# A recurrence swept twice over its chunks: first sweep without a loop, and the input's products for two steps at a time

## The reference

```python
def _L0_ffn_ref(x, W, V, gamma, beta):
    Wx = jnp.einsum('bti,hi->bth', x, W)
    flat = Wx.reshape(B * T, H)
    mean = jnp.mean(flat, axis=0)
    var = jnp.var(flat, axis=0)
    Wx = ((flat - mean) * jax.lax.rsqrt(var + BN_EPS) * gamma + beta).reshape(B, T, H)
    Vt = V.T

    def step(yt, wx_t):
        yt = jax.nn.sigmoid(wx_t + yt @ Vt)
        return (yt, yt)
    ...
    _, ys = jax.lax.scan(step, y0, jnp.swapaxes(Wx, 0, 1))
    return jnp.swapaxes(ys, 0, 1)
...
t = t + _L0_ffn_ref(_ln_t(t), ...)
```

## Time and profile before

| | us |
|---|---|
| median of three runs | 303.04 |
| the three runs | 302.4, 303.04, 312.51 |
| span of the profiled execution (first to last instruction) | 300.2 |
| PE busy over the span | 231.0 |
| DVE busy | 223.3 |
| POOL busy | 150.0 |
| ACT busy | 117.7 |

### The profile page before, as it was taken

The page is one execution under the profiler, slowest core; times in us unless marked ns, Lnnn a source line. Parts: engine busy times, 40 slices in busy tenths (PEclk is TensorE's granted clock), DMA queues, the critical chain, the costliest instruction groups (busy, mean ns, idle before and its releaser), DMA issues.

```text
span 300.2 us, 4789 instructions
## 1 busy us (share of the span) xinstructions
PE 231.0 (77%) x1649; PEld 163.7 (55%) x1649; DVE 223.3 (74%) x384; ACT 117.7 (39%) x227; POOL 150.0 (50%) x223
## 2 busy tenths in 40 slices
PE   0285896868099799997969999795129999889893
PEld 0174782534044399995757869794119972333331
DVE  4999648978778600497893556899997999898893
ACT  3353533343423155555644637752303341231210
POOL 4443881368600088420519469945933528875100
PEclk9999996877789999999998999999655556999999
DMA  6200000000000000000000000000006982868311
GB/s 210 85 15 2 2 2 0 0 1 2 0 0 0 0 0 3 0 2 2 1 2 0 2 0 1 2 2 1 0 0 146 204 196 62 204 182 185 122 37 70
DMA packets 6636, 13.10 MB, mean 44 GB/s; under 512 B 2774, under 2 KB 3030, under 8 KB 6614
## 3 DMA queue, kind: packets, MB, share of 16 engines
q1 hardware_dynamic: 6470, 12.81, 16.8%
q10 hardware_dynamic: 144, 0.01, 0.0%
HBM read 2.32 MB, written 2.10 MB: 15 GB/s over the span
## 4 chain that ended last, share of the span: by engine, by line
DVE 40%; PE 36%; POOL 8%; issue 7%; ACT 5%; DMA 2%; DVEq 1%; SPq 1%; POOLq 0%; ACTq 0%
PE ps L1065 4%; PE ps L1061 4%; DVE var L372 4%; DVE sums L334 4%; PE ps L1483 3%; PE ps L654 3%; POOL x L875 3%; PE ps L1350 3%; PE ps L1368 2%; DVE gated L1958 2%; DMA raw<-in_L_conv_gi_b_dram 2%; PE ps L1248 2%; DVE squares L2094 2%; DVE xn L644 2%; PE ps L1462 1%
## 5 line engine op out<-in xcount | busy, mean ns | idle before, releaser
L654 PE MATMUL ps<-ident,xn 128*128 128x128 f32 x144 | 29.8, 345 | 20.0 <-DVE xn L644 10.5
L654 PEld LDWEIGHTS ps<-ident,xn 128*128 128x128 f32 x144 | 20.8, 179 | 32.8 <-issue 10.3
L875 POOL TENSOR_TENSOR x<-x,sg 128x512 f32 x16 | 22.0, 1390 | 9.2 <-DVE sg L2015 7.7
L1137 PE MATMUL ps<-ones_b,ones_h 128*128 128x512 bf16 x53 | 16.6, 465 | 10.4 <-ACT v_wrap L1584 7.5
L1958 DVE TENSOR_TENSOR gated<-ps,sg 128x512 f32 (+1 forms) x16 | 16.5, 1042 | 10.6 <-ACT sg L1635 10.5
L1098 ACT ACTIVATE gated_t<-ps,bn 128x128 f32<-128x128 f32 x54 | 16.9, 364 | 13.8 <-PE ps L1065 12.9
L372 DVE TENSOR_REDUCE var<-squares 128x32 f32<-128x1024 f32 (+1 forms) x18 | 19.6, 1090 | 2.2 <-ACT squares L340 1.4
L663 ACT ACTIVATE xt<-ps 128x512 f32<-128x512 f32 (+1 forms) x24 | 12.4, 525 | 22.1 <-PE ps L654 17.0
L1462 PE MATMUL ps<-gated,pick 96*128 96x512 bf16 x64 | 20.3, 427 | 0.1
L340 ACT ACTIVATE squares<-x 128x1024 f32<-128x1024 f32 x12 | 12.7, 1056 | 14.8 <-POOL x L875 11.2
L334 DVE TENSOR_REDUCE sums<-x 128x32 f32<-128x1024 f32 x12 | 14.5, 1211 | 4.2 <-DMA x<-in_x_dram 2.9
(11 more groups left out here) (282 smaller groups left out, 632.9 us busy)
## 6 DMA issues: line engine op xcount, KB each, us to landing
out_gate<-gated SPq DMA_DIRECT2D x32, 128.0 KB, 2.3
x<-gated SPq DMA_DIRECT2D x32, 128.0 KB, 2.4
x<-in_x_dram SPq DMA_DIRECT2D x4, 512.0 KB, 5.9
out_dram<-x SPq DMA_DIRECT2D x8, 256.0 KB, 2.0
e_full<-in_L_ffn_expert_b_dram SPq DMA_DIRECT2D x12, 1.0 KB
mask_a<-in_L_conv_mask_dram SPq DMA_DIRECT2D x1, 64.0 KB, 6.8
mask_c<-in_L_conv_mask_dram SPq DMA_DIRECT2D x1, 64.0 KB, 1.8
w_x<-in_L_ffn_expert_w_dram SPq DMA_DIRECT2D x1, 32.0 KB
```

The costliest lines, as they stand in the source:

```text
L654: ins = pe.transpose(bank(s)[:, t * P:(t + 1) * P], xn[:, s, t, :], ident[:, :])
L875: pool.tensor_tensor(v, v, sg[:, s, :], ALU.add).then_inc(pj.added, 1)
L1137: pe.matmul(bank(b).rearrange("p (k o) -> p k o", o=P), ones_h[:, :], ones_b[:, :].unsqueeze(1).to_broadcast([P, GROUP, P]), start=True, s ...
```

## The change

On TensorE both sweeps get code of their own. An input product takes two steps of one stream at once: 256 columns, written to the two halves of one bank (`pair_input`, `summed_at`); a stream's two banks alternate from pair to pair. The state products stay as they were, with 128 columns each. After both state products of a step one pair is issued, for stream 0 and stream 1 in turn (`pair_steps`). The first sweep has no loop any more. In the second sweep the pairs for steps 0 and 1 of both streams stand ahead of the wait for the first sweep's last states. ScalarE's activations keep their order and number and read the new places (`pairs_act`). The repeat loop keeps `sweep_pe` and `sweep_act`, which lose what only the two sweeps needed.

```diff
-        def sweep_pe(pe, stepped, state, base, first=False, begun=None, after=None):
+        def sweep_pe(pe, stepped, state, base):
...
-            begin = FIRST + 1 if first else 1
-            if not first:
...
-            if after:
-                for k in range(1, CHUNK):
-                    step(k, k % 2)
-                    if k in after:
-                        after[k]()
-                return
-            step(begin, begin % 2)
-            with pe.Fori((begin + 1) // 2, CHUNK // 2) as it:
...
+        def pair_at(k, begin):
+
+            n = k - begin
+            return 1 - (n // 2) % 2, P * (n % 2)
+
+        def summed_at(st, k, begin):
+
+            b, at = pair_at(k, begin)
+            return bank(2 + 2 * st + b)[:, at:at + P]
+
+        def pair_input(pe, st, k, begin):
+
+            n = min(2, CHUNK - k)
+            b, at = pair_at(k, begin)
+            pe.matmul(bank(2 + 2 * st + b)[:, 0:n * P], w_bs[:, :],
+                      x_cm[:, CHUNK * st + k:CHUNK * st + k + n, :].rearrange("p a i -> p (a i)"), start=True,
+                      stop=False, skip_group_check=True)
+
+        def pair_state(pe, st, k, begin, base):
+
+            pe.wait_ge(s_state[st], base + k)
+            pe.matmul(summed_at(st, k, begin), v_t[:, :], y_cm[:, CHUNK * st + k - 1, :], start=False,
+                      stop=True, skip_group_check=True).then_inc(s_step[st], 1)
+
+        def pair_steps(pe, k, begin, base, after={}):
+
+            for j in range(k, CHUNK):
+                st = (j - begin) % 2
+                for t in range(2):
+                    pair_state(pe, t, j, begin, base)
+                ahead = j - st + 2
+                if ahead < CHUNK:
+                    pair_input(pe, st, ahead, begin)
+                if j in after:
+                    after[j]()
+
+        def first_sweep_pe(pe):
+
+            k = FIRST + 1
+            for st in range(2):
+                pair_input(pe, st, k, k)
+                pair_state(pe, st, k, k, -FIRST)
+            pair_input(pe, 0, k + 2, k)
+            pair_steps(pe, k + 1, k, -FIRST)
+
+        def second_sweep_pe(pe, after):
+
+            last = y_cm[:, 2 * CHUNK - 1, :]
+            for st in range(2):
+                pair_input(pe, st, 0, 0)
+            for st in range(2):
+                pe.wait_ge(s_state[st], SWEPT)
+            pe.matmul(summed_at(0, 0, 0), v_next[:, :], last, start=False, stop=False, skip_group_check=True)
...
+            pair_input(pe, 0, 2, 0)
+            pair_steps(pe, 1, 0, SWEPT, after)
...
-            sweep_pe(pe, s_step, s_state, -FIRST, True)
+            first_sweep_pe(pe)
...
-            sweep_act(act, s_step, s_state, -FIRST, FIRST + 1)
-            sweep_act(act, s_step, s_state, SWEPT, kept=lambda: act.wait_ge(ends_kept, 1))
+            pairs_act(act, FIRST + 1, -FIRST)
+            pairs_act(act, 0, SWEPT, kept=lambda: act.wait_ge(ends_kept, 1))
```

More of the change, by code:

```diff
@@ L1082, in sweep_pe @@
-            if after:
-                for k in range(1, CHUNK):
-                    step(k, k % 2)
-                    if k in after:
-                        after[k]()
-                return
-            step(begin, begin % 2)
-            with pe.Fori((begin + 1) // 2, CHUNK // 2) as it:
+            last = y_cm[:, 2 * CHUNK - 1, :]
+            for st in range(2):
+                pe.matmul(summed(st, 0, 0), w_bs[:, :], x_cm[:, CHUNK * st, :], start=True, stop=False,
+                          skip_group_check=True)
@@ new lines, in sweep_pe @@
+            pe.matmul(summed(0, 0, 0), v_next[:, :], last, start=False, stop=False, skip_group_check=True)
+            pe.matmul(summed(0, 0, 0)[:, 1:P], v_wrap[:, :], last[:, 0:P - 1], start=False, stop=True,
+                      skip_group_check=True).then_inc(stepped[0], 1)
+            pe.matmul(summed(1, 0, 0), v_t[:, :], y_cm[:, CHUNK - 1, :], start=False, stop=True,
+                      skip_group_check=True).then_inc(stepped[1], 1)
+            step(1, 1)
+            with pe.Fori(1, CHUNK // 2) as it:
@@ L1090, in sweep_pe @@
                 for b in range(2):
                     step(2 * it + b, b)
-        def sweep_act(act, stepped, state, base, first=0, kept=None, looped=False):
+        def pair_at(k, begin):
[10 more added lines that the diff above has]
+                      stop=False, skip_group_check=True)
@@ new lines, in first_sweep_pe @@
+        def first_sweep_pe(pe):
[6 more added lines that the diff above has]
+        def second_sweep_pe(pe, after):
+            last = y_cm[:, 2 * CHUNK - 1, :]
+            for st in range(2):
+                pair_input(pe, st, 0, 0)
+            for st in range(2):
+                pe.wait_ge(s_state[st], SWEPT)
+            pe.matmul(summed_at(0, 0, 0), v_next[:, :], last, start=False, stop=False, skip_group_check=True)
+            pe.matmul(summed_at(0, 0, 0)[:, 1:P], v_wrap[:, :], last[:, 0:P - 1], start=False, stop=True,
+                      skip_group_check=True).then_inc(s_step[0], 1)
+            pe.matmul(summed_at(1, 0, 0), v_t[:, :], y_cm[:, CHUNK - 1, :], start=False, stop=True,
+                      skip_group_check=True).then_inc(s_step[1], 1)
+            pair_input(pe, 0, 2, 0)
+            pair_steps(pe, 1, 0, SWEPT, after)
@@ L1095, in step, with pairs_act, sweep_act @@
+        def pairs_act(act, begin, base, kept=None):
+            for k in range(begin, CHUNK):
+                if kept and k == CHUNK - 1:
+                    kept()
+                for st in range(2):
+                    act.wait_ge(s_step[st], base + k + 1)
+                    act.activation(y_cm[:, CHUNK * st + k, :], summed_at(st, k, begin), ACT.Sigmoid,
+                                   bias=bn[:, 9:10]).then_inc(s_state[st], 1)
+        def sweep_act(act, stepped, state, base):
             def step(k, b):
@@ L1099, in step @@
                                    ACT.Sigmoid, bias=bn[:, 9:10]).then_inc(state[st], 1)
[L1101 to L1109, removed]
+            with act.Fori(0, CHUNK // 2) as it:
+                for b in range(2):
+                    step(2 * it + b, b)
         def keep_ends(dve, signal):
@@ L1269, in _ @@
             pe.wait_ge(bn_dve, 4)
-            def first_swept():
-                for st in range(2):
-                    pe.wait_ge(s_state[st], SWEPT)
-            sweep_pe(pe, s_step, s_state, -FIRST, True)
+            first_sweep_pe(pe)
             def turn_y(q, st):
@@ L1290, in turn_quarter @@
                 turn_y(q, 1).then_inc(y_turn, 1)
-            sweep_pe(pe, s_step, s_state, SWEPT, begun=first_swept,
-                     after={GROUP * (q + 1): lambda q=q: turn_quarter(q) for q in range(QUARTERS - 1)})
+            second_sweep_pe(pe, {GROUP * (q + 1): lambda q=q: turn_quarter(q) for q in range(QUARTERS - 1)})
             for st in range(2):
@@ L1614, in _ @@
                     act.wait_ge(ends_again, n + 1)
-                    sweep_act(act, r_step, r_state, n * CHUNK, looped=True)
+                    sweep_act(act, r_step, r_state, n * CHUNK)
             def copy_c(g, s, early):
```

## The result

The changed kernel takes 300.33 us on the median of 17 runs, the kernel before 302.22 of 17 taken beside them.

The account below looks back on a forecast made before the run. A ring of waits, 0.945 us per written-out step, was taken to bound the scan, above PE's 0.89. Loop 1.17 saved, hand-over 0.10 lost, transposes 0.03 saved: 1.1 off 303.04 gives 301.9 us, range 300.6 to 303.4 (0.80).

Parts of the forecast that it names:

- The ring: Both sweeps: activation, signal, weight loads and passes with drain set 0.945 us per written-out step, above PE's 0.89.
- The pair's price: Scan on PE: a 256-column input product takes 0.435 us, against 0.445 for two of 128 columns.
- The first rival: Input products: cost goes per instruction, not per column; 1.1 us more gain, 300.8 us; chance 0.06.
- the fourth: Input products: a pair is much dearer, at worst 0.78 us, 7.8 together, 309.7 us; chance 0.04.
- The second: Both sweeps: PE sets 0.945; steps would fall to about 0.88, 1.4 us more gain, 300.5 us; chance 0.05.
- the third: First sweep: gaps come from code supply, not the loop, so straight code waits too; 302.8 us; chance 0.05.
- The loop: First sweep without branch and register steps: ten steps take 9.82 us instead of 10.99, 1.17 saved.
- the start: First sweep: pairs ahead of step 6 make the first activation distance 1.31 us, not 0.945.
- the hand-over: Between the sweeps: pairs ahead of the wait make the distance 1.59 us against 1.49, 0.10 lost.
- the transposes: Second sweep: merging shortens the three stretches with transposes by 0.01 us each, 0.03 in all.
- Downstream I take the shift whole.: After the scan: the whole 1.1 us saved comes off the end, with no other wait becoming late.
- The starting value: Whole kernel: median 303.04 us before the change, 2.84 above the profiled span of 300.2, taken as constant.

Follow-up runs that it names:

- the doubled pairs: Changed kernel with every input product issued twice, the second over the first: 310.98 us (one run), scan 40.1 us.
- the run without inputs: Changed kernel with all input products left out of both sweeps from step 5 on: 303.63 us (one run), scan 34.0 us.
- the filled pair of kernels: Kernel before and changed kernel, each with nine useless 512-column products in the third layer's TensorE gap: 301.28 and 300.24 us.
- the delayed one: Changed kernel with five useless 512-column products between its sweeps, 1.1 us later: 302.59 us, ratio 1.0022 to before; with the gap filled 300.78 us.
- A delay of 0.65: Changed kernel with three useless products between its sweeps: 300.21 us, ratio 0.9927 to before.
- the kernel written out alone: Kernel before with the first sweep written out, input products still single, second sweep unchanged: 299.72 us, ratio 0.9891 to before.
- pairs in the second sweep: Kernel before with 256-column input products in the second sweep alone, first sweep in its loop: 302.49 us, ratio 1.0001 to before.

## Why the prediction was wrong

*The ring.* Right: 0.945 in both sweeps, with pairs, with singles, without input products at full clock, and beaten by PE alone once PE's work was 1.31.

*The pair's price.* Right: 0.43 in the chain, 0.435 forecast. The first rival (per instruction) is refuted by the doubled pairs, and so is the fourth (dearer pairs). The second (PE sets 0.945) is refuted by the run without inputs, the third (code supply) by the written-out steps at 0.945 with no gap. In the first rival's sum the hand-over would have been 0.09 shorter, not longer; its 1.1 has it so.

*The loop, the start, the hand-over, the transposes.* Right, to 0.02 us each: 9.83 for 9.82, 1.60 for 1.59, 1.80 for 1.80. The scan is 1.1 us shorter, as summed.

*"Downstream I take the shift whole."* This is the step that failed for the gain. I checked there only who waits and whether a cover holds, all in microseconds of queues. What stands downstream at a fixed distance also meets the granted clock, and that was not in the sum: a stretch of half clock behind an idle gap of 2.3 us, 20 us after the scan, worth 1.3 to 1.5 in the profiles that have it (40.0 and 39.8 against 38.5). The rows for it were in the trace of before: the clock in windows there is 0.52, and the products behind it take 1.91, where their neighbours take 1.03. I had read the clock in the two sweeps alone, where it is 1.00.

*The starting value.* The forecast took "2.84 us above that span, which I take as constant", that is, the median of three runs, 303.04. This term was too large: wherever a run's time and its own span are both on record, they are 1.7 to 2.4 us apart, most often 1.8, and the median of 17 runs of before is 302.22. That is half of the 1.6 us between the forecast, 301.9, and the result. From 302.22 the same sum gives 301.1, and the same range, 0.8 lower (299.8 to 302.6), would have held the result although the gain was wrong.

*The size.* The gain was off by 1.5 us by the ratio, by 0.8 by the medians; the filled pair of kernels differs by about the 1.1 forecast. Shown: half clock follows the gap in four of the eight profiles without filling and in none of the four with it, the filling takes 1.2 and 1.8 us off the means of the kernel before and of the delayed one, a delay of 1.1 us brings the loss back, and the filling then takes it away again. Not shown: why the gap draws the half clock in most executions of one kernel and in few of another. A delay of 0.65 did nothing, and the kernel written out alone, whose scan is shorter still, had it in its one profile. No rule by the gap's place comes out of these runs; a forecast could only have widened its range by these 1.5 us.

## What to carry to other kernels

Find what sets the distance of the steps before pricing the work in them: here a ring of waits with 0.06 us of room, so merging products gave nothing, and the loop's overhead was the whole gain of the scan. When a change shifts everything behind it, read the granted clock of all later stages in the trace of before; wherever it is low behind an idle gap, put the price of that stretch into the range on both sides. Take the starting value from more than three runs when it scatters by as much as the gain. And hidden work can pay: products that nobody needs, put into an idle gap, made the kernel before 1.2 +- 0.4 us faster.

## What was not expected of the hardware

A gap of 2.27 us on TensorE, behind 2.8 us in which it was busy all the time, was met by 3.4 us at 0.50 of the clock in four profiles (before, written out alone, pairs in the second sweep, 1.1 us later) and by none in four others with the same idle time (changed, 0.65 us later, no inputs, pairs twice). The fall came just before PE resumed (a mean of 0.96 over the 2.34 us up to 157.31 is 0.19 us at 0.50) or 1.0 to 1.5 us after (in the delayed kernel at 158.3, where PE had resumed at 156.96).

With two state products per step and no input products, the granted clock fell to 0.50 at 107.7 and stayed there for 20.5 us, of which PE is shown busy 19.83; from 128.2 to the end of the scan it was 1.00 with the same two products per step and the transposes between. There a PE shown busy was no sign of the level it ran at.

The start of the program to w_bs, the same code everywhere, took 103.9 to 106.9 us in twelve profiles, with 17 to 24 us of it at half clock, in places that differ from profile to profile. This scatter is larger than the change itself, which is why stretches of one profile were needed here beside the means.
